# Full attention of a fused two-layer network: value sums taken for eight slots at a time, with a ring of twelve exponentials and value tiles of 17 columns a head

## What is computed

```
q, k = rope(x @ Wq.T + bq), rope(x @ Wk.T + bk)     # x: the normalised tokens
v    = x @ Wv.T + bv
p    = exp((q @ k.T) / 4 - shift)                   # shift: maximum of the row, cancels below
out  = ((p @ v) / sum(p)) @ Wo.T + bo               # added to the residual
```

## Time and profile before

| | |
|---|---|
| median of 3 runs | 4232.3 us (4220.6 to 4237.8) |
| profiled execution | 4227.6 us, its span 4225.8 us |
| mean granted TensorE clock | 0.941 of 2.4 GHz |
| busy over the span | PE 86%, VectorE 69%, ScalarE 45%, GpSimd 38% |
| values groups (line 2655) | first at 3361.2 us, last ends at about 3917 us |
| scores and maxima (lines 2643, 2633) | 512 matmuls each |
| reductions (line 2846) | 512, 681 ns median |
| exponentials (line 2777) | 512, 600 ns mean |

### The profile page before, as it was taken

The page is one execution under the profiler, slowest core; times in us unless marked ns, Lnnn a source line. Parts: engine busy times, 40 slices in busy tenths (PEclk is TensorE's granted clock), DMA queues, the critical chain, the costliest instruction groups (busy, mean ns, idle before and its releaser), DMA issues. The chain is left out here.

```text
span 4225.8 us, 60116 instructions
## 1 busy us (share of the span) xinstructions
PE 3651.5 (86%) x19256; PEld 2610.1 (62%) x19256; DVE 2897.8 (69%) x5457; ACT 1910.7 (45%) x3895; POOL 1618.8 (38%) x1493
## 2 busy tenths in 40 slices
PE   4888878998499999998899579788788899999998
PEld 3555567887387888877778534444556455554666
DVE  5787556665576666646655467787789767666898
ACT  3555634333355555545344244443223266666332
POOL 3776626443566666524544211010101354441000
PEclk8999978999799999998899889989999899999999
DMA  5999802554200000001355400000300444441000
GB/s 136 298 276 254 278 32 87 165 155 150 68 17 17 19 19 19 17 2 49 115 162 170 145 20 21 10 20 1 61 0 13 96 106 107 101 112 34 11 15 15
DMA packets 228874, 358.33 MB, mean 85 GB/s; under 512 B 36482, under 2 KB 132851, under 8 KB 221811
## 3 DMA queue, kind: packets, MB, share of 16 engines
q1 hardware_dynamic: 204038, 265.38, 21.3%
q0 software_dynamic: 24544, 89.36, 8.7%
HBM read 173.82 MB, written 172.20 MB: 82 GB/s over the span
## 5 line engine op out<-in xcount | busy, mean ns | idle before, releaser
L2846 DVE TENSOR_REDUCE ab_nmx<-banks 128x1 f32<-128x512 f32 x512 | 329.2, 684 | 135.7 <-PE banks L2633 132.8
L2777 ACT ACTIVATE ab_pt<-banks 128x512 f32<-128x512 f32 x512 | 283.0, 600 | 160.8 <-PE banks L2643 152.1
L1712 POOL TENSOR_TENSOR lb_pq<-lb_pq,lb_rr 128x512 f32<-128x512 f32 x192 | 206.3, 1077 | 307.1 <-DVE lb_rr L1579 303.9
L1454 ACT ACTIVATE lb_pq<-banks,lb_nmx 128x256 f32<-128x256 f32 x384 | 178.5, 470 | 229.2 <-DVE lb_nmx L1574 226.0
L2643 PE MATMUL banks<-ab_qT,ab_kT 128*128 128x512 f32 x512 | 251.5, 496 | 5.3 <-ACT ab_pt L2777 5.3
L1574 DVE TENSOR_REDUCE lb_nmx<-banks 128x2 f32<-128x512 f32 x192 | 131.1, 683 | 157.4 <-PE banks L1306 156.2
L358 ACT ACTIVATE da_pt<-banks 128x512 f32<-128x512 f32 (+1 forms) x384 | 179.3, 537 | 127.7 <-PE banks L270 123.4
L2633 PE MATMUL banks<-ab_kT,ab_qT 128*128 128x512 f32 x512 | 207.6, 409 | 18.4 <-DVE ab_nmx L2846 17.0
L644 POOL DMA_INDIRECT mb_xi<-moe_ys,moe_b_place x64 | 65.0, 1015 | 385.8 <-DVE mb_uT L2093 337.9
L285 PE MATMUL banks<-da_pt,da_vx 128*64 128x512 f32 (+3 forms) x1024 | 166.9, 472 | 34.7 <-POOL da_pt L578 31.0
L2422 PE MATMUL banks<-w_f_dT,f_hT 128*128 128x256 f32 x768 | 181.7, 387 | 4.0 <-ACT f_hT L2458 4.0
(11 more groups left out here) (532 smaller groups left out, 11275.7 us busy)
## 6 DMA issues: line engine op xcount, KB each, us to landing
moe_xs<-zero SPq DMA_DIRECT2D x71, 512.0 KB, 10.8
moe_ys<-zero SPq DMA_DIRECT2D x71, 512.0 KB, 11.5
moe_a_w_raw<-in_moe_w SPq DMA_DIRECT2D x48, 512.0 KB, 3.9
moe_b_w_raw<-in_moe_w SPq DMA_DIRECT2D x48, 512.0 KB, 4.0
da_spill<-da_hi SPq DMA_DIRECT2D x128, 128.0 KB, 2.4
ab_spill<-ab_hi SPq DMA_DIRECT2D x128, 128.0 KB, 2.4
ab_qT<-ab_spill POOLq DMA_DIRECT2D x32, 392.0 KB, 5.8
ab_kT<-ab_spill POOLq DMA_DIRECT2D x32, 392.0 KB, 5.5
```

What stands on the lines that cost most here:

```text
L1454: nc.scalar.activation(pq[:, n % RING, t, :], ps[:, S_BANK + n % 2, 2 * P * t:2 * P * t + 2 * P], ACT.Exp, bias=nmx[:, n % RING, t:t + 1], ...
L1712: nc.gpsimd.tensor_tensor(pq[:, n % RING, :, :], pq[:, n % RING, :, :], bcast(rr[:, n % RING, :], 2, 2 * P), ALU.mult).then_inc(s_p, 1)
L2777: nc.scalar.activation(pt[:, s % RING, :], ps[:, EXP_BANK + s % 3, :], ACT.Exp, scale=AB_D ** -0.5).then_inc(s_e, 1)
L2846: nc.vector.tensor_reduce(nmx[:, g % 2, col:col + 1], ps[:, MAX_BANK + n % 3, :], op=ALU.max, axis=AX.X, negate=True).then_inc(s_mx, 1)
```

## The change

Three things. The values are issued for two groups in a row, in every eighth slot (s = 9, 17, 25, ...), and no longer for one group in every fourth. So that the exponentials live long enough, the ring has 12 tiles in place of 8. To make room, a head's value tile has 17 columns in place of 32; the matmul still takes 32 columns, so it reads the 15 first columns of the next head as well, and the sums that these give land in rows that nothing reads.

```diff
-    RING = 8
+    RING = 12
+    VW = AB_D + 1
@@ full_attention
+        columns = [x[:, 0:NT * AB_H * VW].rearrange("p (t h d) -> p t h d", t=NT, h=AB_H) for x in vx]
@@ values (TensorE)
                     for i in range(4):
-                        last = nc.tensor.matmul(ps[32 * i:32 * i + 32, SUM_BANK, :], vx[b % 2][:, j, h + i, :],
+                        first = (j * AB_H + h + i) * VW
+                        last = nc.tensor.matmul(ps[32 * i:32 * i + 32, SUM_BANK, :], vx[b % 2][:, first:first + 32],
                                                 pt[:, (4 * v + i) % RING, :], start=(j == 0), stop=(j == NT - 1))
@@ pe_slots, the loop over the slots
-                    if s >= 5 and (s - 5) % 4 == 0 and (s - 5) // 4 < NV:
-                        values((s - 5) // 4)
+                    if s >= 9 and (s - 9) % 8 == 0 and (s - 9) // 4 < NV:
+                        values((s - 9) // 4)
+                        values((s - 9) // 4 + 1)
@@ act_slots, emptying of "v"
-                        nc.scalar.copy(vx[b % 2][:, 2 * i:2 * i + 2, :, 0:AB_D],
+                        nc.scalar.copy(columns[b % 2][:, 2 * i:2 * i + 2, :, 0:AB_D],
@@ value_columns (GpSimd)
-                    nc.gpsimd.memset(vx[i][:, :, :, 16:17], 1.0)
-                    nc.gpsimd.memset(vx[i][:, :, :, 17:32], 0.0).then_inc(s_vset, 1)
+                    nc.gpsimd.memset(columns[i][:, :, :, AB_D:VW], 1.0)
+                    nc.gpsimd.memset(vx[i][:, NT * AB_H * VW:], 0.0).then_inc(s_vset, 1)
@@ last_stages
-                   sb("vx0", [P, NT, AB_H, 32]))
+                   sb("vx0", [P, NT * AB_H * (AB_D + 1) + 16]))
-        late = (sb("vx1", [P, NT, AB_H, 32]), ..., sb("pt", [P, 8, T]),
+        late = (sb("vx1", [P, NT * AB_H * (AB_D + 1) + 16]), ..., sb("pt", [P, 12, T]),
```

More of the change, by code:

```diff
@@ L3017, in last_stages @@
         scratch = (qf, t1, sb("qs", [P, 2, T]), sb("hi", [P, 2, T], F32R), sb("lo", [P, 2, T], F32R),
-                   sb("vx0", [P, NT, AB_H, 32]))
+                   sb("vx0", [P, NT * AB_H * (AB_D + 1) + 16]))
         with ExitStack() as space:
             first_tiles = FeedForward.tiles(core, space, "f41_")
-        late = (sb("vx1", [P, NT, AB_H, 32]), sb("nmx", [P, 2, 16]), sb("nmT", [16, 2, P], F32R), sb("pt", [P, 8, T]),
+        late = (sb("vx1", [P, NT * AB_H * (AB_D + 1) + 16]), sb("nmx", [P, 2, 16]), sb("nmT", [16, 2, P], F32R), sb("pt", [P, 12, T]),
                 sb("osb", [P, 2, T]), sb("rr", [P, NT, 4]), sb("att", [P, NT, AB_H, AB_D]))
```

## The result

| | before | after |
|---|---|---|
| median of 6 runs | 4227.6 us (4220.6 to 4237.8) | 4253.4 us (4244.7 to 4257.3) |
| ratio | | 1.0057, 95% interval 1.0042 to 1.0072 |
| profiled execution | 4227.6 us, span 4225.8 | 4257.3 us, span 4255.5 |

The changed kernel is slower by 0.57%, 24 us. The forecast was +18 us (+0.4%, 4250 us), on a base of three runs that lay 5 us over the six counted now; on the base counted now it would be 4246 us.

A forecast was written before the change was run, and what follows sets the result against it. TensorE's order was taken to set the time, at most three banks ahead of VectorE. Octets summed to +19 us (4.0 from slots 10 to 17), rounded to +18 on 4232.3: 4250 us, range 4220 to 4268.

The forecast's parts named there:

- change of column width: TensorE's switch between 32 and 128 columns around a values group: 0.34 us, saved once by each of 64 pairs.
- closed seam: Between a pair's two groups: no added time; the rival, a whole change of 0.34 us there, 4268 us, had chance 0.10.
- group hidden in a wait: Slots 18 to 25 and 34 to 41: removing the group brings nothing forward, its streaming returns elsewhere, +0.86 us each.
- slip against full banks: Maxima wait for VectorE to empty three banks: slots 2 to 9 come to +0.09 us, 50 to 57 to -0.10.
- ScalarE in slots 42 to 49: Scores of slot 47 wait for an exponential behind `ab_qf`: slip 0.47 us, octet +0.13.
- Slots 58 to 65: Eight slots without a values group: gain 0.34 us, slip 0.97 behind VectorE's reductions and slot 61's turn, +0.63 us.
- Slots 10 to 17: Octet hanging on slot 13's turn: +0.86 us where its data are late, elsewhere -0.11; 4.0 us over all frames.
- From slot 475 on: The end of the attention, after the last maxima: taken as no change.
- Slots 26 to 33: Two "v" fills give VectorE time to empty its banks: no slip, -0.34 us.
- The clock: Rival: longer standstills at slots 22 and 38 bring five more clock falls, 1.7 us each, +9, 4260 us; chance 0.20.
- TensorE does not stay the bound: Denies the rival that TensorE bounds all through, 64 x 0.34 us saved, 4211 us; chance 0.08.
- only the hidden groups count: Rival: bank slips are small, 18 octets cost 0.86 us, 46 gain 0.34, sum 0, 4232 us; chance 0.20.

The follow-up runs named there:

- E6: Changed kernel's order, but VectorE reduces only 128 of the 512 columns of a maxima bank; ratio 0.9999 to the kernel before.
- E2: Ring and packing as changed, pairs only where slots 21 and 37's groups move to 25 and 41, others single; ratio 1.0062 to the kernel before.
- E1: Ring of twelve and packed value tiles alone, values in single groups every four slots as before; ratio 0.9996 to the kernel before.
- E3: Changed kernel with pairs only at slots 1, 9, 33, 49 and 57, single groups at 13, 21 and 37; ratio 1.0002 to the kernel before.
- E7: Changed kernel with the turn of slot 61 moved to slot 57; ratio 1.0052 to the kernel before.
- E4: Ring and packing as changed, pairs only at slots 33 and 57 (up to slot 33 of frame 6), others single; ratio 0.9984 to the kernel before.
- E5: Ring and packing as changed, single groups, VectorE reducing only 128 of the 512 columns of a maxima bank; ratio 0.9966 to the kernel before.
- E8: E4's kernel (pairs only at slots 33 and 57) with the turn of slot 61 moved to slot 57; ratio 0.9993 to the kernel before.
- E9: E2's kernel run again, unchanged; 4241.8 us in one run, beside a median of 4221.4 us for the kernel before.
- E10: E4's kernel run again, unchanged, with the turn left in slot 61; ratio 0.9995 to the kernel before.

## Why the prediction was right, and where not

**Right, as worked out.** The cost of a change of column width (0.34 us: E6 gains 0.31 to 0.34 where nothing else limits) and the closed seam (1.85 us for a pair). That a group hidden in a wait brings nothing forward when it is taken out, and costs its streaming where it goes: +0.86 and +0.82 measured, shown alone by E2. The slip against full banks in slots 2 to 9 and 50 to 57, to 0.01 us, with the reason shown by E6. ScalarE in slots 42 to 49 (+0.14). Ring and packing at nothing (E1); only the count was off, as GpSimd writes 64 columns of ones and 16 of zeros, not 80 of ones.

**Wrong in size.**
- *Slots 58 to 65*, +0.63 forecast, +1.13 measured. The step that failed is "then slot 61's turn at 3.17; then 3.80": I gave the turn its usual length, 0.63 from its start to the next reduction's. It took 1.22 us, as it came into a running GpSimd instruction. I had such a duration in hand (1.76 us) and read it as late data.
- *Slots 10 to 17*, +4.0 us forecast for all frames, -3.1 measured. I took the waits for the turn's data as fixed. They are not: in E3, where slots 58 to 65 are longer, they vanish, in E7, where these are short again, they are back. 1.6 us or so of the -3.1 are a fall of the clock that stood at slot 17 of frame 6 before and not after. A second error goes the other way: the least length grew by 0.29, where I had -0.11. The group of slot 13 was partly hidden even where the data are in time: the "shift" fill came forward by 0.58 us, against 0.86 for the group in slot 17.
- *From slot 475 on*, taken at nothing, +3.0 us measured. With no maxima in the way ScalarE sets the pace, and while a pair of 1.85 us runs it works off its three banks and stops. About 1 us of it is the clock: the fall around slot 502 lasted 6.8 us in place of 3.4. With single groups there and the long fall (E1, E4, E5, E8, E9) it is +0.8 to +1.5, with the short one (E2, E10) nothing, with pairs and the long one (E3, E6, E7) +3.1 to +3.4. So the pairs cost some 2 us.
- *Slots 26 to 33*, -0.34 forecast, -0.28 measured.

**The clock.** My rival had five more falls. Behind frame 0, the profiled execution has four in slots 10 to 25, all of them in slots 18 to 25; before had two, one there and one at slot 17. Two more are about 3 us. In slots 18 to 25 it is three more, about the 4.6 us by which they are over the forecast (10.6 us measured, 7 x 0.86 = 6.0 forecast). TensorE stands at least 1.65 us at slot 22 in each of frames 1 to 6, and the clock fell in four of them. So this rival is partly true, beside the forecast and not in its place: E2 and E9 show two and six for one kernel. It is one reason why these kernels scatter and why single profiles mislead.

The other rivals fell. TensorE does not stay the bound (E6 against the changed kernel). The slips against the banks are not small: "only the hidden groups count" had every other pair gain 0.34, -13 us for E3, and E3 has none of it; slots 2 to 9, 42 to 49 and 58 to 65 came out longer. The seam costs nothing.

That the sum was so near is partly luck, as errors went against each other: +3.0 (slots 58 to 65, six frames), +3.0 (the end), +4.6 (slots 18 to 25, the clock), -0.5 (slots 34 to 41) and -7.1 (slots 10 to 17).

## What to carry to other kernels

Putting like work together saves changes of mode, but makes longer bursts: ask how far each engine can run ahead of the others (here three banks, 1.4 us of TensorE's work against 1.8 us of VectorE's), and how long a stretch between two bursts may get before they run full. Four slots cost nothing here, eight did. Before moving work, look whether it stands in a wait: there it is free, and anywhere else it costs its length. If a wait hangs on a chain that starts earlier in the same loop, expect part of any gain or loss on the way to be given back, and count it over a whole turn of the loop.

## What the runs showed of the hardware

A VectorE instruction with both operands in SBUF (the turn, 0.68 us) that starts while GpSimd's TENSOR_TENSOR runs is done only 0.55 us after that one ends: started 3653.45, GpSimd's end at 3652.83 + 1.29 = 3654.12, its own at 3654.67. The Trainium skill, page "GPSIMD Engine Reference", section "Specifications", lists the SBUF interfaces as shared with VectorE, with contention for VectorE instructions of two SBUF inputs; the trace agrees. When GpSimd's instruction starts second, it is the one that waits. In the kernel before, the turn of the same slot started 0.11 us ahead of the same GpSimd instruction; it kept its 0.68 us, and GpSimd's took 1.72 in place of 1.29:

```profile
3636.26 0.68 DVE L2832 TENSOR_TENSOR ab_qs<-ab_qs,w_ab_sinT 128x512 f32<-128x512 f32 x1
```

```profile
3636.37 1.72 POOL L2892 TENSOR_TENSOR ab_t<-ab_qf,w_ab_cosT 128x512 f32<-128x512 f32 x1 [0.16 <-issue]
```

But coming first is not always enough while GpSimd issues a DMA. In slot 13 of frame 0 the turn started 0.48 us ahead of GpSimd's TENSOR_TENSOR, during such an issue, and it was done 0.56 us behind its end, after 2.32 us:

```profile
3373.68 2.32 DVE L2832 TENSOR_TENSOR ab_qs<-ab_qs,w_ab_sinT 128x512 f32<-128x512 f32 x1 [5.17 <-DMA ab_qs<-ab_qf]
```

```profile
3373.13 1.02 POOL L2916 DMA_DIRECT2D ab_kT<-ab_spill  x2 [7.38 <-DMA ab_spill<-ab_lo]
3374.16 1.28 POOL L2892 TENSOR_TENSOR ab_t<-ab_qf,w_ab_cosT 128x512 f32<-128x512 f32 x1
```

In frame 1 the turn (at 3441.63) starts during such an issue too and keeps its 0.69 us; what decides isn't shown. VectorE's reductions from PSUM were not slowed: in the changed kernel 104 of them start while a GpSimd TENSOR_TENSOR runs, and they take 673 to 692 ns, as all 512 do (673 to 693).

Two tiled groups in a row run without a gap: a round of four fp32 matmuls with 32 columns and 512 moving takes 0.43 us in the third and fourth round too (in the pair shown above the rounds start at 3648.43, 3648.88, 3649.31 and 3649.74).
